# Four conditioned residual layers in one kernel: the residual adds of L1 to L3 moved into the diagonals of the matrices, and x2 computed transposed

## The reference, cut to what matters

```python
x = x + L0(x, ..., itok_B_2_6)     # gate/up/silu/down MLP with per-batch low-rank adapters
x = x + einsum('bct,bcd->bdt', x, W1[itok_B_0_15])            # L1: a 32x32 mix of the rows of a batch
x = x + base + 2 * lora            # L2: base = x @ W.T; logits = x @ Wr.T + 5 * onehot(language);
                                   # top 2 of 8 experts, softmax gates, h = x @ A.T, lora = (h * gates) @ B.T
x = x + einsum('bct,bcd->bdt', x, W3[itok_B_0_15])            # L3: as L1, other weights
```

## Time and profile before

| what | us |
|---|---|
| median of 3 runs | 654.25 (652.68 to 658.75) |
| profiled execution, span from first to last instruction | 656.1 |
| TensorE busy with products, share of the span | 615.8 (94%) |
| VectorE busy | 300.1 (46%) |
| ScalarE busy | 202.5 (31%) |
| GpSimd busy | 210.0 (32%) |

### The profile page before, as it was taken

One profiled execution on the slowest core, in us unless ns is written; L12 is line 12 of the kernel. 1 busy time (PEld: TensorE's weight loads), 2 busy tenths in 40 slices (PEclk: granted clock), 3 DMA queues, 4 the chain that ended last, 5 costly groups with the idle time before them and its releaser, 6 DMA issues.

```text
span 656.1 us, 11454 instructions
## 1 busy us (share of the span) xinstructions
PE 615.8 (94%) x4659; PEld 599.5 (91%) x4659; DVE 300.1 (46%) x748; ACT 202.5 (31%) x514; POOL 210.0 (32%) x230
## 2 busy tenths in 40 slices
PE   4798998999999999999998999899987999999997
PEld 4797998999899899999998999899987998898985
DVE  3576543243333333333233323332331346889897
ACT  3464422231223122313231323132311333333331
POOL 4348341114111501151115111511164512656551
PEclk9899999999999989999999899999997999999998
DMA  6775042114212411141124011401134111131212
GB/s 201 251 257 160 30 136 85 39 34 131 75 39 65 126 47 39 65 141 33 39 65 157 17 39 65 157 17 39 33 129 129 39 33 49 50 97 65 96 49 81
DMA packets 26613, 55.80 MB, mean 85 GB/s; under 512 B 4224, under 2 KB 7744, under 8 KB 26560
## 3 DMA queue, kind: packets, MB, share of 16 engines
q1 hardware_dynamic: 18608, 31.17, 14.0%
q0 software_dynamic: 7808, 23.86, 12.0%
q10 hardware_dynamic: 144, 0.03, 0.0%
HBM read 46.66 MB, written 8.39 MB: 84 GB/s over the span
## 4 chain that ended last, share of the span: by engine, by line
PE 79%; DVE 9%; issue 6%; POOL 2%; ACT 1%; DMA 1%; SPq 1%; POOLq 0%; DVEq 0%; ACTq 0%
PE gu_ps L1031 15%; PE gu_ps L1030 15%; PE gu_ps L1029 15%; PE down_ps L1030 7%; PE down_ps L1029 7%; PE down_ps L1031 7%; DVE route L930 2%; PE l_ps L1031 2%; PE l_ps L1029 2%; PE l_ps L1030 2%; DVE x L948 1%; DVE wgu_sb L881 1%; POOL a_raw L563 1%; PE x2t_ps L1137 1%; PE tg_ps L1029 1%
## 5 line engine op out<-in xcount | busy, mean ns | idle before, releaser
L1029 PE MATMUL gu_ps<-xt,wgu_sb 128*128 128x256 f32 (+1 forms) x704 | 203.2, 289 | 9.3 <-DVE wgu_sb L881 8.3
L1031 PE MATMUL gu_ps<-xt,wgu_sb 128*128 128x256 f32 (+1 forms) x704 | 202.9, 288 | 5.0 <-issue 4.7
L1030 PE MATMUL gu_ps<-xt,wgu_sb 128*128 128x256 f32 (+1 forms) x704 | 202.5, 288 | 3.2 <-issue 3.1
L857 DVE TENSOR_TENSOR act<-act,gu_ps 128x256 f32<-128x256 f32 (+1 forms) x88 | 37.0, 420 | 243.2 <-ACT act L681 238.0
L1029 PEld LDWEIGHTS gu_ps<-xt,wgu_sb 128*128 128x128 f32 (+1 forms) x704 | 136.5, 194 | 11.6 <-DVE wgu_sb L881 8.3
L1031 PEld LDWEIGHTS gu_ps<-xt,wgu_sb 128*128 128x128 f32 (+1 forms) x704 | 136.8, 194 | 5.7 <-issue 5.7
L1030 PEld LDWEIGHTS gu_ps<-xt,wgu_sb 128*128 128x128 f32 (+1 forms) x704 | 136.5, 194 | 2.0 <-issue 2.0
L563 POOL DMA_INDIRECT b_sel_raw<-b_gu,idx_rank x48 | 46.2, 963 | 259.5 <-PE gu_ps L1031 243.6
L681 ACT ACTIVATE act<-gu_ps 128x256 f32<-128x256 f32 (+1 forms) x88 | 33.7, 383 | 289.8 <-PE gu_ps L1031 223.9
L1029 PE MATMUL down_ps<-wd_sb,act_hl 128*128 128x288 f32 (+1 forms) x352 | 104.8, 298 | 3.4 <-POOL wd_sb L625 1.9
L1031 PE MATMUL down_ps<-wd_sb,act_hl 128*128 128x288 f32 (+1 forms) x352 | 104.3, 296 | 2.8 <-issue 2.8
(11 more groups left out here) (132 smaller groups left out, 1019.1 us busy)
## 6 DMA issues: line engine op xcount, KB each, us to landing
wgu_sb_raw<-wgu SPq DMA_DIRECT2D x20, 256.0 KB, 5.2
xt_raw<-x_t SPq DMA_DIRECT2D x16, 256.0 KB, 3.1
x_res<-x_rows SPq DMA_DIRECT2D x8, 512.0 KB
x_after_l<-x_res SPq DMA_DIRECT2D x8, 512.0 KB
x<-x_after_l SPq DMA_DIRECT2D x16, 256.0 KB
out<-y SPq DMA_DIRECT2D x15, 256.0 KB, 2.1
wd_sb_raw<-wd SPq DMA_DIRECT2D x10, 256.0 KB, 5.6
w_raw<-w2ra_t SPq DMA_DIRECT2D x1, 1296.0 KB
```

Of the source, the lines that this page charges most:

```text
L857: ve.tensor_tensor(act[0:k, s % 2, :], act[0:k, s % 2, :], gu_ps[s % GU_BANKS][0:k, 1, :], ALU.mult).then_inc(s_mul, 1)
L1029: pe.matmul(out_, stationary[0], moving[0], start=start, stop=False, skip_group_check=True)
L1030: pe.matmul(out_, stationary[0], moving[1], start=False, stop=False, skip_group_check=True)
L1031: return pe.matmul(out_, stationary[1], moving[0], start=False, stop=stop, skip_group_check=True)
```

## The change

The residual adds disappear as instructions. GpSimd adds an identity to every 32x32 block of W1 and W3 (`add_eyes`, one instruction over the 1024 gathered columns, from a new constant "eye_ch"); VectorE adds an identity to the four diagonal 128x128 blocks of L2's W (`fold_identity`), before they are split. So (I + W1), (I + W) and (I + W3) are applied and each product yields the whole next x.

`l1`, `add_x2` and `transpose_x2` become `mixed_transpose`: for each of the four 128-column chunks, x1's chunk is the stationary operand and the block-diagonal matrix the moving one, 3 products of 128 columns, 12 in all, and x2 comes out transposed. x2 and x3 no longer lie in SBUF: x3's high part is copied by ScalarE from the L2 bank in PSUM, its low part is computed by VectorE from PSUM (no longer by GpSimd), and y is a copy by ScalarE (the last 256 columns of the last tile by VectorE). L3 gets two PSUM banks in turn.

```diff
@@ TensorE
-            def l1(t):
+            def mixed_transpose(t):
+
                 pe.wait_ge(s_x1lo, t + 1)
-                ...
-                mix(l1_of(t), t, 0, x1_hl).then_inc(s_l1, 1)
-
-            def transpose_x2(t):
-                pe.wait_ge(s_x2, t + 1)
                 if t >= 1:
                     pe.wait_ge(s_x2tlo, t)
                 for c in range(HC):
-                    mm = pe.transpose(x2t_ps[:, c, :], x2[:, t % 3, c * P:(c + 1) * P], ident)
+                    cols = slice(c * P, (c + 1) * P)
+                    mm = product(x2t_ps[:, c, :], (x1_hl[:, t % 2, 0, cols], x1_hl[:, t % 2, 1, cols]),
+                                 (bd13_hl[:, t % BD, 0, 0, :], bd13_hl[:, t % BD, 1, 0, :]), c == 0, c == HC - 1)
                 mm.then_inc(s_x2t, 1)
@@ l2_base
                     if t >= 2:
-                        pe.wait_ge(s_x3, t - 1)
+                        pe.wait_ge(s_x3lo, t - 1)
                         pe.wait_ge(s_hg, t - 1)
@@ l3
-                elif t >= 1:
-                    pe.wait_ge(s_y, t)
+                if t >= 2:
+                    pe.wait_ge(s_y, t - 1)
@@ TensorE's tile loop
                 if i + 1 < NT:
-                    transpose_x2(i + 1)
+                    mixed_transpose(i + 1)
...
-                if i + 2 < NT:
-                    l1(i + 2)
@@ VectorE
+            def low_x3(t):
                 for n, (a, b) in enumerate(pieces(t)):
                     ve.wait_ge(s_x3hi, t + n + 1)
+                    ve.tensor_tensor(halves(x3_hl[:, t % 2, 1, :], a, b), base_of(t, a, b),
+                                     halves(x3_hl[:, t % 2, 0, :], a, b).bitcast(F32), ALU.subtract).then_inc(s_x3lo, 1)
+            def fold_identity():
+
+                ve.wait_ge(s_w, 32)
+                for c in range(HC):
+                    at = c * L2_COLS + c // 2 * L2_WIDTH[0] + c % 2 * P
+                    ins = ve.tensor_tensor(w_raw[:, at:at + P], w_raw[:, at:at + P], ident, ALU.add)
+                ins.then_inc(s_fold, 1)
@@ VectorE's tile loop
+            for i in range(1, NT + 1):
+                low_hgt(i - 1)
+                if i < NT:
                     route_top(i)
+                if i < NT - 1:
+                    low_x2t(i + 1)
+                if i < NT:
                     route_gates(i)
+                low_x3(i - 1)
+            copy_last_y()
@@ ScalarE
+                    sc.wait_ge(s_l2, t + n + 1)
+                    sc.copy(halves(x3_hl[:, t % 2, 0, :], a, b), base_of(t, a, b)).then_inc(s_x3hi, 1)
+            def copy_y(t):
+                a, b = pieces(t)[0]
+                if t >= 2:
+                    sc.wait_ge(s_out[t % 2], 16 * (t // 2))
+                sc.wait_ge(s_l3, t + 1)
+                sc.copy(y[:, t % 2, a:b], l3_of(t, 0)).then_inc(s_y, 1)
@@ ScalarE's tile loop
+            for i in range(NT + 3):
+                if 1 <= i <= NT:
                     high_hgt(i - 1)
                 if i < NT:
                     exponential(i)
+                if i >= 3:
+                    copy_y(i - 3)
                 if 1 <= i < NT - 1:
+                    high_x2t(i + 1)
+                    if i + 2 < NT:
+                        highs(i + 2)
+                if 1 <= i <= NT:
                     high_x3(i - 1)
@@ GpSimd
+            def add_eyes(a, b):
+
+                w = w13_raw[:, a:b, :].rearrange("p t (m d) -> p t m d", m=2)
+                pool.tensor_tensor(w, w, const("eye_ch").unsqueeze(1).unsqueeze(2).to_broadcast([P, b - a, 2, CH]),
+                                   ALU.add).then_inc(s_eye, b - a)
+                pool.wait_ge(s_eye, b)
```

More of the change, by code:

```diff
@@ L94, in const_array @@
         "is_ch": p[:, None] // CH == np.arange(TB)[None, :],
+        "eye_ch": p[:, None] % CH == np.arange(CH)[None, :],
         "row_rank": (p % RANK)[:, None],
@@ L281, in bass_conditioned_residual_chain @@
         hgt_ps = ps("hgt_ps", [H])
-        l1_ps = ps("l1_ps", [H])
-        l3_ps = ps("l3_ps", [H])
+        l3_ps = [ps(f"l3_ps{i}", [H]) for i in range(2)]
         x2t_ps = ps("x2t_ps", [HC, P])
@@ L643, in _ @@
             lows(2)
[L644 to L650, removed]
+            for t in range(3, NT):
+                block_diagonals(t)
+                lows(t)
         @block.scalar
@@ L941, in low_hgt, with copy_last_y @@
                                  ALU.subtract).then_inc(s_hgtlo, 1)
[L943 to L953, removed]
+            def low_x3(t):
                 for n, (a, b) in enumerate(pieces(t)):
                     ve.wait_ge(s_x3hi, t + n + 1)
[L956 to L966, removed]
+                    ve.tensor_tensor(halves(x3_hl[:, t % 2, 1, :], a, b), base_of(t, a, b),
+                                     halves(x3_hl[:, t % 2, 0, :], a, b).bitcast(F32), ALU.subtract).then_inc(s_x3lo, 1)
+            def copy_last_y():
+                t = NT - 1
+                a, b = pieces(t)[1]
+                ve.wait_ge(s_out[t % 2], 16 * (t // 2))
+                ve.wait_ge(s_l3, t + 2)
+                ve.tensor_copy(y[:, t % 2, a:b], l3_of(t, 1)).then_inc(s_ylast, 1)
+            def fold_identity():
[4 more added lines that the diff above has]
+                ins.then_inc(s_fold, 1)
             ve.memset(warm[:], 0.0).then_inc(s_warm, 1)
@@ L993, in _ @@
                     ve.tensor_scalar(lang5[:], lang5[:], LANG_BIAS, None, ALU.mult).then_inc(s_lang, 1)
[L994 to L1000, removed]
-            for i in range(NT + 2):
-                if 1 <= i <= NT:
-                    low_hgt(i - 1)
-                if i == NT:
-                    add_y(NT - 3)
-                if 1 <= i < NT:
+                if s in (STEPS - 2, STEPS - 1):
+                    low_x2t(s - (STEPS - 2))
+            for i in range(1, NT + 1):
+                low_hgt(i - 1)
+                if i < NT:
                     route_top(i)
-                if i == NT - 1:
+                if i < NT - 1:
+                    low_x2t(i + 1)
+                if i < NT:
                     route_gates(i)
-                if 1 <= i and i + 1 < NT:
-                    low_x2t(i + 1)
-                if 1 <= i <= NT:
-                    add_x3(i - 1)
-                if i == NT:
-                    low_last_x3()
-                if 1 <= i < NT - 1:
-                    route_gates(i)
-                if 1 <= i and i + 2 < NT:
-                    add_x2(i + 2)
-                if i >= 2 and i != NT - 1:
-                    add_y(i - 2)
+                low_x3(i - 1)
+            copy_last_y()
         @block.tensor
@@ L1146, in l2_base @@
                     if t >= 2:
-                        pe.wait_ge(s_x3, t - 1)
+                        pe.wait_ge(s_x3lo, t - 1)
                         pe.wait_ge(s_hg, t - 1)
-                if t == 1 and half == 0 and c0 == 0:
-                    pe.wait_ge(s_x2, 3)
                 for c in range(c0, c1):
```

57 lines of the change are left out of this document (14 added, 43 removed).

## The result

| | before | after |
|---|---|---|
| median of 4 runs, us | 654.24 (652.68 to 658.75) | 704.59 (703.55 to 713.1) |
| span of the profiled execution, us | 656.1 | 702.4 |

The ratio of the times is 1.0775, 95% interval 1.0719 to 1.0832: the change makes the kernel 7.8% slower. The forecast was 692, in a range of 674 to 710.

What follows compares the result with a forecast made beforehand. TensorE bounds the kernel before; the change closes a chain of 9.2 us a turn. 548.4 + 14 x 9.2 + 11.8 = 689.0 us, with the clock 694.2, less 1.9 gives 692; range 674 to 710.

Steps and rivals of the forecast that it cites:

- part 2: Tile loop: x3's low part, behind the gates, closes a chain between upper halves; period 9.2 us against 6.57.
- Narrow products: TensorE, tile loop: 12 products of 128 moving columns at 0.115 us each, 1.38 us a tile.
- The line through wider products: Lower bound for a narrow product, drawn through 512 and 328 columns: 0.063 us at 128, 0.75 us a tile.
- The hold of the gates: VectorE, tile loop: GpSimd instructions hold four of six small gate operations; gates take 2.4 us, against 1.31 free.
- Rival 1: Tile loop: chain closes but shorter, gates not held or narrow products at 0.063; period 8.1, 674 us; chance 0.18.
- TensorE's work and gap: Tile loop: TensorE's own work is 6.6 us of each 9.2 us turn, so it idles 2.6 us.
- Rival 3: Tile loop: TensorE remains the bound, x3's low part never the last wait; period 5.9, 641 us; chance 0.04.
- Start and tail: Around the loop: tile 1's upper half starts at 548.4; from tile 15's upper half to the end, 11.8 us.
- The identity adds: GpSimd's and VectorE's sums outside the loop cost nothing, covered by idle time; without cover 1 to 3 us once.
- part 3: TensorE's clock falls in four of 14 gaps of 2.6 us, 1.3 us each: 5.2 us; bounds none and 24 us.
- rival 2: Tile loop longer: narrow products at 0.233, 710 us, or clock falling in nearly every gap, 702 us; chance 0.19.
- The time around the span: Whole kernel: 1.9 us taken off, as the earlier median 654.25 lay below the profiled span of 656.1.

Runs made afterwards that it cites:

- experiment 5: experiment 1's order, with narrow products of 64 instead of 128 moving columns from tile 3 on (output differs): 646.04 us, 1.0246 of before on the second chip.
- Experiment 2: Changed kernel, with GpSimd's subtractions for tile i+2 made to wait for hg of tile i: 674.51 us, 1.0255 of before.
- experiment 1: Changed kernel, with VectorE's low part of x3 of tile i-1 moved ahead of the gates of tile i: 669.15 us, 1.0192 of before.
- experiment 3: Changed kernel, with 13 unused products behind L3 in each turn to fill TensorE's gap: 693.23 us, 1.0530 of before.
- experiment 7: Changed kernel, with x3's low part before the gates, experts before L2's second six products, tile 1's narrow products one step later: 635.14 us, 1.0090 of before, second chip.

## Why the prediction was right, and where it missed

The mechanism was the one predicted. The turn from 610.51 to 619.77 against part 2, in us from the start of the upper half:

| point of the chain | predicted | measured |
|---|---|---|
| hg's transpose (612.38) | 1.9 | 1.87 |
| first narrow product (613.37) | 2.95 | 2.86 |
| ScalarE's high part of x2t (614.86) | 4.5 | 4.35 |
| VectorE's low part of x2t (615.55) | 5.2 | 5.04 |
| the gates (616.16) | 5.8 | 5.65 |
| hg (618.78) | 8.2 | 8.27 |
| the next upper half (619.77) | 9.2 | 9.26 |

- **Narrow products**: 0.115 taken, 0.11 measured ((614.55 - 613.37) / 11 = 0.107 in this turn). The line through wider products, 0.063, is no price for a narrow one: from 128 to 64 columns the columns don't count, as experiment 5 shows. The Trainium skill, "TensorE: Matmul & The Clock Gate", section "LDWEIGHTS (loading the stationary operand)", gives a load as its columns over 1.2 GHz, an estimate of 0.107 for 128; the trace agrees, with 128 and with 64 moving columns. The figure of the same page's "Back-to-back issue gap", 0.081, doesn't fit these products; the measurement decides.
- **The hold of the gates**: 2.4 taken, 2.62 measured. The price was right, the picture a little off: I had four of the six operations held, while nearly all of the hold (1.12 of 1.33) falls on one, L922, which GpSimd's 1.28 us subtraction keeps. Experiment 2 shows the cause. Rival 1 (gates not held) falls with it, and so does its other half, products at 0.063.
- **TensorE's work and gap**: 6.6 and 2.6 taken, 6.64 and 2.62 measured. Rival 3 asked for a chain under 6.57; even experiment 1's is 7.45.
- **Start and tail**: 548.4 and 11.8 predicted, 548.83 and 11.9 measured. The start is partly luck: the wait at 533 was not in my sum, and the same L0 ended 3 us later in experiment 3. I had followed the transposes' place in the loop over tiles, but not in L0's last steps, where the narrow products stand one step earlier than the second tile's transposes did. The identity adds were hidden, as forecast (TensorE has no idle time from 494 to 530 us). GpSimd's:

```profile
504.63 2.41 POOL L609 TENSOR_TENSOR w_raw<-w_raw,const_sb 128x1024 f32<-128x1024 f32 x1 [1.64 <-DMA w_raw<-w,idx_ch]
```

- **The clock, the step that failed in size** (part 3): I took four slow stretches of 1.3 us, 5.2. Eight turns are 1.39 to 1.56 longer than 9.26, 11.8 us, and the last, slow as well, brings it to nine stretches; with the other small differences the 14 turns are 141.65 - 14 x 9.26 = 12.0 over the chain. The price of one was near, the count was not. I had counted from two gaps near the start, one of which had left the clock alone; the gaps that return in each turn did otherwise. Here rival 2's "nearly every gap" was the nearer reading, 12 x 1.3 = 15.6. Experiment 3 shows that the gap is the cause, and experiments 1 and 2 that gaps of 0.81 and 1.29 leave every turn at full length.
- **The time around the span, the second miss**: I took 1.9 off, because the median of before lay 1.9 under the profiled span. Executions of the changed kernel last about 1.9 longer than their span (704.27 for 702.4), so against the span the forecast had to add 1.9: 3.8 us. If the same holds before the change, the profiled execution there (656.1 + 1.9 = 658.0) was near the slowest of its runs, and taking 1.9 off was a fair step to a typical one; but the changed kernel's profiled run, a typical one by its time, starts tile 1 at 548.83, as late as that slow one (549.16). Why isn't shown. The span itself was missed by 702.4 - 694.2 = 8.2: 6.8 of clock, 14 x 0.06 = 0.8 of chain, 0.4 at the start, 0.1 in the tail. Together 12.0 of the miss of 12.6; the rest is rounding and the spread of the runs.

## What to carry to other kernels

Before you shorten an engine's list, look at which entry of it frees a buffer for somebody else, and keep that entry ahead of the long dependent work; here moving one line (1.81 us a turn) outweighed all the adds that were saved. Work taken from engines that are busy 30 to 46% gained nothing here, where TensorE is the bound; what took its place could only be hidden or cost. And a gap that returns in every turn can cost more than its length, since the clock may come down with it: here the gaps of 2.62 us cost 12 us more over 14 turns, those of 0.81 and 1.29 us nothing more.

## What the runs showed of the hardware that was not expected

- Filling an idle gap with useless products made the kernel 11 us faster (experiment 3): the clock stayed up, and the products of the chain all ran at full speed.
- The slow turns come in a pattern of three (9.26, 10.8, 10.66). What sets it was not tried.
- A product with 64 moving columns follows the last as late, 0.11 us, as one with 128 (experiment 5).
- GpSimd's 1.28 us subtraction holds a VectorE operation of one element per partition for its whole length, while VectorE's low part of x3, which reads PSUM, keeps its 0.69 us under the same subtraction (experiment 1, L941 at 607.38 and GpSimd's L603 from 606.74 to 608.02). The Trainium skill, "SBUF — State Buffer", section "Who interferes with whom", has both; the trace agrees. In the changed kernel L920 and L921, with one input each, keep 0.14 and 0.16 under GpSimd's L600 (615.83 to 616.57).
- The same program ran 4% faster on the second chip (629.74 against 657.84). The difference is in L0, which these experiments leave as it is: with the same order the 14 turns of the loop take 104.4 us on the first chip and 104.5 on the second (experiments 1 and 5), but tile 1 starts at 548.46 and at 525.71. In 100 us of L0 the trace has fewer products on the first chip (experiment 1, then experiment 7), with short gaps that the profile puts down to "issue". Their cause is open.

```profile
100.00:200.00 100.00, 97.39 (x785) 97.07 (x786) 34.40 (x78) 27.68 (x73) 18.26 (x19) 1.00 0.19 59
```
```profile
100.00:200.00 100.00, 100.00 (x813) 100.00 (x813) 35.06 (x80) 28.69 (x76) 19.34 (x20) 1.00 0.19 59
```
